# A conditioned adapter on one core: the stores of D's second half cut into quarters, and three output units moved behind the last pair of sums

## The reference

```python
dWd = ((h @ Wdd.T + bdd) * 0.1).reshape(B, 128, 512)     # Wdd: [65536, 128], 32 MB
dWu = ((h @ Wdu.T + bdu) * 0.1).reshape(B, 512, 128)     # Wdu: [65536, 128], 32 MB
down = relu(einsum('bld,bnd->bln', x, Wd + dWd) + bd)
up = einsum('bln,bdn->bld', down, Wu + dWu) + bu
return x + up
```

## Time and profile before

| | |
|---|---|
| median of 3 runs | 222.43 us (222.25 to 222.94) |
| the profiled execution's own time | 223.91 us |
| its span, first to last instruction | 222.1 us |
| PE / DVE / ACT / POOL busy | 158.6 / 174.2 / 47.1 / 61.5 us |
| DMA | 85.35 MB, mean 384 GB/s |
| stores in the profile | 4 of 1,024 KB, 8 of 512 KB |

### The profile page before, as it was taken

One profiled execution on the slowest core, in us unless ns is written; L12 is line 12 of the kernel. 1 busy time (PEld: TensorE's weight loads), 2 busy tenths in 40 slices (PEclk: granted clock), 3 DMA queues, 4 the chain that ended last, 5 costly groups with the idle time before them and its releaser, 6 DMA issues.

```text
span 222.1 us, 2814 instructions
## 1 busy us (share of the span) xinstructions
PE 158.6 (71%) x1036; PEld 87.5 (39%) x1036; DVE 174.2 (78%) x118; ACT 47.1 (21%) x85; POOL 61.5 (28%) x41
## 2 busy tenths in 40 slices
PE   1063473936564583594998879998799999999940
PEld 0000121211121020143765457664576555597930
DVE  2875979899989999929665967959699999865840
ACT  2000011000010101041432334423342443441000
POOL 1000000000000000026553645555452587872000
PEclk9999587697589659979999999999999999999995
DMA  5999999999999999999999999999999999996398
GB/s 207 419 358 410 431 420 407 375 392 361 413 429 423 409 391 419 426 423 422 416 425 419 422 422 418 423 419 419 412 379 360 388 370 423 390 362 212 131 339 285
DMA packets 20403, 85.35 MB, mean 384 GB/s; under 512 B 1572, under 2 KB 10792, under 8 KB 11176
## 3 DMA queue, kind: packets, MB, share of 16 engines
q1 hardware_dynamic: 20392, 85.21, 96.4%
HBM read 76.81 MB, written 8.39 MB: 384 GB/s over the span
## 4 chain that ended last, share of the span: by engine, by line
PE 36%; DMA 29%; DVE 22%; SPq 5%; issue 4%; ACT 0%; DVEq 0%
DMA w<-in_L_cond_Wdu_dram 21%; DVE wt L260 20%; PE acc L448 16%; PE bank L531 13%; DMA w<-in_L_cond_Wdd_dram 8%; SPq L211 3%; PE dn L511 2%; PE gt L459 2%; PE bank L501 1%; DVE wd_b L267 1%; SPq L188 1%; SPq L210 0%; DVE xs L316 0%; PE bank L475 0%; SPq L206 0%
## 5 line engine op out<-in xcount | busy, mean ns | idle before, releaser
L260 DVE STREAM_TRANSPOSE wt<-w 128x2048 f32<-128x2048 f32 x64 | 144.7, 2293 | 23.4 <-DMA w<-in_L_cond_Wdu_dram 16.7
L448 PE MATMUL acc<-wt,st 128*32 128x512 f32 x512 | 75.1, 712 | 50.2 <-DVE wt L260 50.1
L424 POOL TENSOR_TENSOR xs<-xs,bu_all 128x1024 f32<-128x1024 f32 x16 | 37.8, 2365 | 128.4 <-PE bank L501 128.4
L448 PEld LDWEIGHTS acc<-wt,st 128*32 128x32 f32 x512 | 15.1, 120 | 90.6 <-DVE wt L260 48.4
L511 PE MATMUL dn<-xt,wd_b 128*128 128x256 f32 x128 | 30.6, 382 | 0.6 <-DVE wd_b L269 0.6
L531 PE MATMUL bank<-wu_b,down 128*128 128x128 f32 (+1 forms) x192 | 30.4, 313 | 0.0
L531 PEld LDWEIGHTS bank<-wu_b,down 128*128 128x128 f32 x192 | 26.1, 191 | 6.3 <-issue 5.0
L429 POOL TENSOR_TENSOR xs<-up_s,xs 128x512 f32<-128x512 f32 x18 | 22.6, 1280 | 10.7 <-ACT up_s L387 10.7
L342 ACT ACTIVATE g_rows<-acc 128x512 f32<-128x512 f32 x16 | 9.6, 597 | 74.5 <-PE acc L448 74.5
L511 PEld LDWEIGHTS dn<-xt,wd_b 128*128 128x128 f32 x128 | 23.0, 190 | 4.1 <-issue 0.8
L370 ACT ACTIVATE xt<-bank 128x512 f32<-128x512 f32 x32 | 17.4, 595 | 18.2 <-PE bank L501 18.2
(11 more groups left out here) (21 smaller groups left out, 13.9 us busy)
## 6 DMA issues: line engine op xcount, KB each, us to landing
w<-in_L_cond_Wdd_dram SPq DMA_DIRECT2D x32, 1024.0 KB, 7.4
w<-in_L_cond_Wdu_dram SPq DMA_DIRECT2D x32, 1024.0 KB, 10.0
xs<-in_x_dram SPq DMA_DIRECT2D x8, 1024.0 KB, 12.2
out_dram<-xs SPq DMA_DIRECT2D x4, 1024.0 KB, 10.0
out_dram<-xs SPq DMA_DIRECT2D x8, 512.0 KB, 5.4
down<-in_L_cond_Wd_dram SPq DMA_DIRECT2D x1, 256.0 KB, 7.1
down<-in_L_cond_bdd_dram SPq DMA_DIRECT2D x1, 256.0 KB, 7.3
down<-in_L_cond_Wu_dram SPq DMA_DIRECT2D x1, 256.0 KB, 11.6
```

What stands on the lines that cost most here:

```text
L260: nc.vector.transpose(wt[:, tslot].rearrange("p r (k j) -> p k r j", j=QUAD), w[:, slot, :].rearrange("p (k r h) -> p k r h", r=R, h=QUAD) ...
L424: nc.gpsimd.tensor_tensor(xs[:, b, i0:i0 + UNIT_I], xs[:, b, i0:i0 + UNIT_I], bu_pair, ALU.add).then_inc(bu_added, 1)
L448: last = nc.tensor.matmul(a[TILE * place:TILE * (place + 1)], st[:, r, low * TILE:(low + 1) * TILE], wt[:, slot + h, r], start=low == 0 an ...
```

## The change

Each unit of columns 256 to 511 is stored by itself, as its own unit is finished: 16 stores of 256 KB, in runs of 128 columns. The wait for unit v is GpSimd's counter for unit 16 and VectorE's for units 17 to 31. GpSimd's share falls from 18 to 17 units. PE's order changes: units 17, 18 and 19 no longer stand before the last pair's sums; unit 17 stands between the sums and `turn_group`, where unit 20 stood, and 18, 19 and 20 behind the turn.

```diff
-POOL_UNITS = 18
+POOL_UNITS = 17
...
-UP_COUNT = (2, 1, 2, 1, 2, 1, 2, 1, 2, 1, 3)
+UP_COUNT = (2, 1, 2, 1, 2, 1, 2, 1, 2, 1, 2)
...
-UP_BEFORE_LAST = 20
-UP_BEFORE_TURN = 21
+UP_BEFORE_TURN = 18
...
-            sp.wait_ge(pool_final, POOL_UNITS)
-            for v in range(UP_UNITS - QUARTER_UNITS, UP_UNITS):
-                sp.wait_ge(dve_final, v - POOL_UNITS + 1)
-                b, rows, _ = unit_at(v)
-                sp.dma_start(out_rows[b, :, rows, HALF:D], xs[:, b, rows, HALF:D]).then_inc(out_stored, 16)
+            for v in range(HALF_UNITS, UP_UNITS):
+                if v < POOL_UNITS:
+                    sp.wait_ge(pool_final, v + 1)
+                else:
+                    sp.wait_ge(dve_final, v - POOL_UNITS + 1)
+                b, rows, cols = unit_at(v)
+                sp.dma_start(out_rows[b, :, rows, cols], xs[:, b, rows, cols]).then_inc(out_stored, 16)
                 stores += 1
...
-                if t == CHUNKS - PAIR:
-                    for v in range(POOL_UNITS, UP_BEFORE_LAST):
-                        up_unit(v)
...
                 if t == CHUNKS - 1:
-                    for v in range(UP_BEFORE_LAST, UP_BEFORE_TURN):
+                    for v in range(POOL_UNITS, UP_BEFORE_TURN):
                         up_unit(v)
```

## The result

The changed kernel takes 219.83 us (218.94 to 221.36, 6 runs) against 222.34 (221.78 to 222.94): ratio 0.9887, 95% interval 0.9847 to 0.9927. That is 2.5 us faster, and the forecast was 2.6. The profiled execution took 221.36 us with a span of 219.1; before, it was 223.91 with 222.1. So the span fell by 3.0 us and the execution's own time by 2.55: what lies around the span grew from 1.8 to 2.3 us, which the experiments come back to. Two later series of the same kernel gave 220.29 (ratio 0.9898, 0.9848 to 0.9947) and 220.04 (0.9869, 0.9820 to 0.9918). The ratios leave out the executions of the slow state, 1.5% or more above the fastest of the same kernel, so they can differ a little from the quotient of the medians shown.

The account below looks back on a forecast made before the run. Taken as the bound: 4 MB of stores that could not begin before 207.9 us. Late engine 204.8 + 16 x 0.88 = 218.9, plus 0.2 and 0.4, gives span 219.5 against 222.1; 2.6 off the median 222.43 is 219.8, range 217.7 to 221.5.

Parts of the forecast that it names:

- The gap and its cause: Stores' tail: DMA engines idle from 203.4 to 208.7 us because SP waits 8.4 us for unit 24; early small stores fill it.
- The move: PE's order: last pair's sums 2.3 us earlier, three more units behind them, last addition 0.4 us later, hidden under the stores.
- D: Time the 16 DMA engines need for one 256 KB store in 512 B runs: 0.88 us, between 0.835 and 0.93.
- The line through the 8 KB loads and the 1 KB stores: Upper bound of D from packet times: 36.9 ns per 1,000 B plus 10.2 ns fixed, so 281 GB/s, 0.93 us.
- The late DMA engine: One DMA engine finishes batch 3's first half at 204.8, others at 203.4; the 16 small stores are counted from 204.8.
- The floor of the engines: End set by supply: unit 31 issued at 214.5 lands 2.35 us later, end 217.3, 2.2 us under the sum.
- The rate in bytes: Rival, chance 0.10: 512 B store packets keep 341 GB/s, 0.77 us per 256 KB, time 218.0 us.
- the rate in packets: Rival, chance 0.09: a store packet costs 48 ns whatever it holds, 1.54 us per 256 KB, time 230.3 us.
- SP's issue as the bound: Rival, chance 0.04: each issue costs SP 1.31 to 1.37 us, 14 stores take 19 us, end 225.
- no effect at all: Rival, chance 0.03: DMA engines gain the gap and lose it to packet price, D 1.0 to 1.09, about 222 us.
- The 2.0 us: Fixed part of each DMA in the skill page; in series 16 x 2.6 = 42 us, a reading the prediction rejected as overlapped.

Follow-up runs that it names:

- stores_only: The kernel before with only the new loop of 16 small stores, old order of PE and GpSimd's 18 units: 219.33 us, ratio 0.9846 to before.
- move_only: The changed kernel with the old loop of eight 512 KB stores, so only the unit counts and PE's order differ from before: 223.25 us, ratio 1.0000.
- after_again: The changed kernel unaltered, run in a second series: 220.29 us, ratio 0.9898 to the kernel before.
- skip4: The changed kernel without the stores of units 16 to 19, so 1 MB of output is not written: 219.43 us, ratio 0.9864 to before.
- late_quarters: The changed kernel with two added waits, so no small store is issued before unit 24 is finished: 225.67 us, ratio 1.0114 to before.
- two_queues: The changed kernel with the odd units' stores issued from ScalarE's queue instead of SP's: 219.06 us, ratio 0.9840 to before.

## Why the prediction was right

**The gap and its cause.** Right. The wait for unit 24 held 4 MB; the first small store was issued at 199.25 and the DMA engines did not stop. `stores_only` and `move_only` show that this part alone is the gain.

**The move.** Right inside the span: the pair's sums came directly behind the last transpose with PE idle for 0.38 us (0.3 forecast), and the last addition ended 16.8 us behind that transpose, where it was 16.5 (0.3 later; 0.4 forecast). Over all profiles that distance is 16.8 to 18.3 us with the move and 16.5 to 17.8 without, so the 0.3 of this one pair is not resolved. Inside the span the move is worth nothing measurable, as forecast. Around the span it costs 0.4 us, which the prediction put at nothing when it took the difference of the spans off the median.

**D.** Mis-sized a little: 0.88 forecast, 0.90 measured (291 GB/s in the profile after; 286 to 289 in four others, so up to 0.92). The line through the 8 KB loads and the 1 KB stores had said 281 GB/s, and the loads of 512 B 314; the stores lie nearer the line. It makes 0.4 us over 16 stores.

**The late DMA engine.** Over-sized, and the end behind it under-sized. From the last bytes to the end of the span it was 0.77 us in all fourteen profiles, where 0.6 was forecast. The last large packet of batch 3 ended at 205.0, 201.6 and 204.2 in the three profiles of the changed kernel, and 16 x 0.904 + 0.8 = 15.3 us behind that would be 220.3, 216.9 and 219.5; the spans end at 219.1, 216.8 and 218.4. So counting from the late engine holds where it is hardly late (`after_again`, 0.6 us) and is 1.1 to 1.2 us too long where it is late by 2.8 or 1.5 us. How a late engine makes up part of its delay stays open. Put on the issue of batch 3's store (198.94 before), the three spans end at 220.0 (219.1 + 0.93), 219.0 (216.8 + 2.22) and 218.9 (218.4 + 0.49), 219.3 in the mean against the forecast 219.5. That is closer than the terms were: too much for the late engine against too little for D and for the end.

**The time.** 219.8 was forecast and 219.83 measured, and to that extent it is luck. The profiled span fell by 3.0 us where 2.6 was forecast, and 0.4 us of that was lost again outside the span.

**The floor of the engines.** Wrong in size: 2.8 us behind the last addition was the forecast, 3.5 was measured in `skip4`. The step that failed is the landing of a 256 KB store: not 3.0 less the missing bytes, 2.35, but 3.0 itself. The trace shows why: 2.5 stores of bytes were still to move when the last one was issued, so it stood behind 1.5 others, while the 3.0 of before had been read from a 512 KB store that met idle engines. The first store of `late_quarters`, 256 KB and idle engines, landed in 2.4 us: the 2.35 was right for that case, and the case was the wrong one. The true distance to the floor was 1.3 to 2.0 us, not 2.2.

**The rivals.** The rate in bytes (341) and the rate in packets (about 170 GB/s) are both refuted by 286 to 291 GB/s; SP's issue as the bound by `two_queues`; no effect at all by intervals that end at 0.995 or below in three series of the changed kernel. The Trainium skill's demand ("DMA: Bandwidth & Descriptors", "Rules for kernel authors") for 1 MiB or more per DMA would have spoken against the change; here 16 stores of 256 KB kept the DMA engines at a share of 1.01, if at 291 GB/s instead of 341. The 2.0 us that the prediction took from that page of the Trainium skill stand there for DMAs issued by GpSimd, and these stores are issued by SP; the sum did not use them.

## What to carry to other kernels

Read the end of the chain against the end of the span: where the engines finish 8 us before it, look for stores that wait for their slowest part, and release each part by its own wait. Price the shorter runs first (here 341 to 290 GB/s for 1,024 to 512 B), and compare the loss over all bytes with the gap that is filled; both can be measured alone, one by holding the small stores back and one by releasing them. Once the stores keep up with the supply within a few per cent, neither larger runs, nor a second queue, nor fewer bytes gave anything that the measurement could tell. And compare the execution's own time with its span on both sides: the stores without the move gave the whole gain without the 0.4 us outside the span.

## What the runs showed of the hardware

A long issue on SP was a wait: 0.37 us with short queues, 0.87 us in a steady backlog (`late_quarters`), where one issue started every 0.92 us, the time that the DMA engines needed for 256 KB at 286 GB/s. With stores of half the run length the trace's DMA share stayed at 1.0 while the rate fell by 15%, so a share near 1 does not give the rate: the run length has to be read beside it. Packets of 512 B went at 286 to 291 GB/s as stores and, in one microsecond of the profile before, at 314 as loads. From the last bytes of the last store to the end of the span it was 0.76 to 0.77 us in all fourteen profiles.
